# Five value groups and new images for q and k in a 16-batch attention and feed-forward kernel on one core

## The reference

```python
qkv = encodings @ attn_w.T + attn_b                      # (16, 256, 384)
q, k, v = jnp.split(qkv by heads, 3, axis=-1)
scores = jnp.einsum('bhki,bhqi->bhkq', k, q) / math.sqrt(8)
scores = jnp.where(mask, scores, -10000.0)               # key <= query
probs = jax.nn.softmax(scores, axis=2)                   # over the keys
combined = jnp.einsum('bhkq,bhkl->bhql', probs, v)
x = layernorm(x + combined @ out_w.T + out_b)
# lhs = x, per row: round(lhs / scale) in -127..127, likewise rhs per column
x = layernorm(x + (q_lhs @ q_rhs) * lhs_scale * rhs_scale)
```

## Time and profile before

| | us |
|---|---|
| median of 3 runs | 268.69 |
| lowest, highest | 267.32, 268.91 |
| profiled execution, its own time | 268.74 |
| its span in the trace | 266.9 |
| TensorE busy | 227.1 |
| VectorE, ScalarE, GpSimd busy | 187.7, 184.8, 129.4 |

### The profile page before, as it was taken

One profiled execution on the slowest core, in us unless ns is written; L12 is line 12 of the kernel. 1 busy time (PEld: TensorE's weight loads), 2 busy tenths in 40 slices (PEclk: granted clock), 3 DMA queues, 4 the chain that ended last, 5 costly groups with the idle time before them and its releaser, 6 DMA issues.

```text
span 266.9 us, 8051 instructions
## 1 busy us (share of the span) xinstructions
PE 227.1 (85%) x2991; PEld 174.3 (65%) x2991; DVE 187.7 (70%) x529; ACT 184.8 (69%) x384; POOL 129.4 (48%) x255
## 2 busy tenths in 40 slices
PE   6366859999999999999999999999999999888710
PEld 3144547778786878687878787878777777666300
DVE  4726866768678787888888888888878878434631
ACT  4895236776877868686868686878787676788420
POOL 7514040506162837474656556564646434455664
PEclk9858798999999999999999999999999999999955
DMA  4397497474747373747566564647464701010001
GB/s 138 121 233 130 131 254 145 141 140 141 143 138 144 100 180 113 162 128 160 141 151 154 141 158 136 145 130 154 150 113 155 127 22 27 18 46 19 22 20 41
DMA packets 50887, 32.77 MB, mean 123 GB/s; under 512 B 7200, under 2 KB 50848, under 8 KB 50848
## 3 DMA queue, kind: packets, MB, share of 16 engines
q1 hardware_dynamic: 50704, 32.06, 49.2%
q10 hardware_dynamic: 144, 0.20, 0.3%
HBM read 17.17 MB, written 14.68 MB: 119 GB/s over the span
## 4 chain that ended last, share of the span: by engine, by line
PE 70%; ACT 10%; issue 5%; DVE 5%; POOL 4%; DMA 4%; SPq 1%; POOLq 0%; ACTq 0%; DVEq 0%
PE pv_bank L902 16%; PE dve_bank L866 14%; PE act_bank L866 12%; PE act_bank L923 5%; PE act_bank L870 5%; PE dve_bank L870 4%; ACT heads_t L525 3%; PE dve_bank L947 3%; PE act_bank L933 3%; PE dve_bank L965 3%; DMA k_stat<-imagek 2%; DVE part_max L670 2%; PE dve_bank L913 1%; PE act_bank L975 1%; ACT k_stat L565 1%
## 5 line engine op out<-in xcount | busy, mean ns | idle before, releaser
L487 ACT ACTIVATE probs<-act_bank 128x512 f32<-128x512 f32 x160 | 96.3, 603 | 46.7 <-PE act_bank L870 42.8
L670 DVE TRANSPOSE_TENSOR_REDUCE part_max<-dve_bank 128x16 f32<-128x512 f32 x160 | 110.4, 707 | 19.1 <-PE dve_bank L870 18.1
L866 PE MATMUL dve_bank<-q_move,k_stat 124*128 124x192 bf16 (+3 forms) x512 | 66.3, 245 | 8.8 <-DMA k_stat<-imagek 7.4
L866 PE MATMUL act_bank<-q_move,k_stat 128*128 128x192 bf16 (+3 forms) x512 | 62.3, 235 | 0.5 <-DMA q_move<-shift 0.5
L866 PEld LDWEIGHTS dve_bank<-q_move,k_stat 124*128 124x128 bf16 x512 | 40.6, 118 | 28.6 <-issue 11.1
L902 PE MATMUL pv_bank<-probs,v_stat 128*32 128x256 f32 (+3 forms) x1024 | 48.7, 305 | 9.1 <-ACT heads_t L525 9.1
L416 POOL TENSOR_TENSOR qk_rest<-qk_f,qk_parts 128x512 f32<-128x512 f32 x15 | 17.5, 1166 | 73.6 <-ACT qk_f L505 73.6
L866 PEld LDWEIGHTS act_bank<-q_move,k_stat 128*128 128x128 bf16 x512 | 43.9, 115 | 2.9 <-DMA q_move<-shift 1.0
L870 PE MATMUL dve_bank<-causal,identb 128*128 128x256 bf16 (+1 forms) x160 | 41.9, 262 | 0.0
L870 PE MATMUL act_bank<-causal,identb 128*128 128x256 bf16 (+1 forms) x160 | 40.7, 254 | 0.0
L902 PEld LDWEIGHTS pv_bank<-probs,v_stat 128*32 128x32 f32 x1024 | 23.9, 109 | 20.3 <-ACT heads_t L525 12.5
(11 more groups left out here) (92 smaller groups left out, 321.9 us busy)
## 6 DMA issues: line engine op xcount, KB each, us to landing
imageq<-qk_parts SPq DMA_DIRECT2D x32, 192.0 KB, 1.9
imagek<-qk_parts SPq DMA_DIRECT2D x32, 192.0 KB, 2.0
q_move<-imageq SPq DMA_DIRECT2D x32, 192.0 KB, 3.9
k_stat<-imagek SPq DMA_DIRECT2D x32, 192.0 KB, 4.3
xt_in<-xt_dram SPq DMA_DIRECT2D x16, 128.0 KB, 4.3
x_in<-x_dram SPq DMA_DIRECT2D x16, 128.0 KB, 3.4
out_dram<-o SPq DMA_DIRECT2D x16, 128.0 KB, 2.0
q_move<-shift SPq DMA_DIRECT2D x32, 8.0 KB
```

The lines of the kernel that those rows point to most:

```text
L487: act.activation(probs[u][:, :], act_bank[at % ACT_BANKS][:, :], ACT.Exp, scale=SCALE).then_inc(act_emptied, 1)
L670: dve.tensor_reduce(out32, dve_bank[at % DVE_BANKS][:, :].rearrange("k (c q) -> k c q", q=32), op=ALU.max, axis=AX.X, apply_transpose=True ...
L866: pe.matmul(bank[:, at:at + TOK - blk * KB], keys, q_move[b % QK_RING][0:rows, p, blk * KB:TOK], start=(at == 0), stop=False, skip_group_c ...
```

## The change

The **images** are new. q's image has three planes (one per part) of 16 x 8 rows, ordered by head-in-pair and depth first and pair second, each of 256 values and 32 of padding. k's image has three planes of the same rows with the keys of both heads, 512 values and 32 of padding; the zeros of the other head are in the image (`zero_image` clears it once). A batch writes a q and a k plane for each part, six copies, and reads two products at a time, 32 rows, in six copies. Where both products use the same part, the source names the plane twice.

**Batch 0** does not go through an image: 12 copies of 16 rows bring it from SBUF to SBUF (`place_first`), k from `k_apart`, in which GpSimd has put the heads apart. Five of these copies are issued by ScalarE.

**q and k** are taken from the banks once, in fp32; GpSimd casts the first part. The weights of q and k are reordered once in SBUF (`wqk`). The third part is made at the start of GpSimd's next phase.

**Order in a phase.** `LEAD` is 6. There are five value groups of two units each. Products in fp32 stand together after units 1, 3, 5, 7 and 9; q and k are projected apart, after units 3 and 5; `project_out` moves one batch earlier, to the end of the phase before. The set-up of the feed-forward weights moves into phase -1. The ones and zeros of the last rows are written by VectorE and ScalarE in place of SyncE's four copies.

```diff
+PRODUCTS = ((0, 0), (2, 0), (0, 1), (0, 2), (1, 0), (1, 1))
+NPROD, ROWS = len(PRODUCTS), 2 * HD
+FIRST_LOADS, READS, WRITES = 2 * NPROD, NPROD, 2 * PARTS
+
+PAD = 32
+Q_PAIR, K_PAIR = TOK + PAD, 2 * TOK + PAD
+K_PLANE = ROWS * PAIRS * K_PAIR
+LAST_ROW, SHIFT_ROW = NPROD * ROWS, 124
...
-LEAD = 8
+LEAD = 6
...
-PV_GROUPS = [(0, 1), (2, 3, 4), (5, 6), (7, 8, 9)]
+PV_GROUPS = [(u, u + 1) for u in range(0, NU, 2)]
...
-ACT_EXTRAS = {0: [("v", 1)], 1: [("zq", -3)], 6: [("q", 4), ("k", 4)], 8: [("heads", -1)]}
-DVE_EXTRAS = {0: [("out", -2)], 4: [("ffn", -3)], 5: [("shift", 1), ("pv", -1)]}
+ACT_EXTRAS = {1: [("v", 1), ("zq", -3)], 3: [("q", 4)], 5: [("k", 4)], 7: [("heads", -1)]}
+DVE_EXTRAS = {4: [("ffn", -3)], 5: [("pv", -1), ("shift", 1)], 9: [("out", -1)]}
...
-        image = [[nc.dram_tensor(f"image{w}{i}", (128, NPROD, TOK), BF16, kind="Internal").ap()
-                  for i in range(QK_RING)] for w in "qk"]
+        q_image = [nc.dram_tensor(f"q_image{i}", (PARTS, ROWS * PAIRS, Q_PAIR), BF16, kind="Internal").ap()
+                   for i in range(QK_RING)]
+        k_image = [nc.dram_tensor(f"k_image{i}", (PARTS * K_PLANE + 2 * TOK,), BF16, kind="Internal").ap()
+                   for i in range(QK_RING)]
...
+        def place_first(eng, product, w):
+
+            q_part, k_part = PRODUCTS[product]
+            row = ROWS * product
+            if w == 0:
+                eng.dma_start(q_move[0][row:row + ROWS, :, :], qk_parts[0][:, q_part, 0, :]).then_inc(first_loaded, 16)
+            else:
+                eng.dma_start(k_stat[0][row:row + ROWS, :, :, :], k_apart[:, k_part, :, :]).then_inc(first_loaded, 16)
...
-            def write_image(b, half):
-
-                if not real(b):
-                    return
-                wait(sp, qk_split, b, 3 + half)
-                if b == 0:
-                    wait_place(sp, act_emptied, ACT_AT, ("k", b))
-                if half == 0:
-                    wait_ring(sp, qk_loaded, b - QK_RING, 4, 4)
-                for w in range(2):
-                    at = RUNS[w][half]
-                    sp.dma_start(image[w][b % QK_RING][:, 3 * half:3 * half + 3, :],
-                                 qk_parts[b % 2][:, at:at + 3, :]).then_inc(image_written[b % QK_RING], 16)
+            def zero_image(i):
+
+                blocks = k_image[i][0:PARTS * K_PLANE].rearrange("(r a q) -> r a q", r=128, q=K_PAIR)[:, :, 0:2 * TOK]
+                sp.dma_start(blocks, warm[:, :].unsqueeze(1).to_broadcast([128, PARTS, 2 * TOK])).then_inc(image_zeroed[i], 16)
+
+            def write_image(b, n):
+
+                if not real(b) or b == 0:
+                    return
+                if n == 0:
+                    wait_split(sp, b, 1)
+                    wait_loaded(sp, b - QK_RING)
+                    if b <= QK_RING:
+                        sp.wait_ge(image_zeroed[b % QK_RING], 16)
+                else:
+                    wait_split(sp, b, 2 + n)
+                half = K_PLANE // 2
+                k = k_image[b % QK_RING][n * K_PLANE:n * K_PLANE + 2 * (half + TOK)].rearrange("(s e) -> s e", s=2)
+                k = k[:, 0:half].rearrange("s (x q) -> s x q", q=K_PAIR)[:, :, 0:TOK]
+                sp.dma_start(q_image[b % QK_RING][n, :, 0:TOK],
+                             qk_parts[b % 2][:, n, 0, :]).then_inc(image_written[b % QK_RING], 16)
+                sp.dma_start(k, qk_parts[b % 2][:, n, 1, :]).then_inc(image_written[b % QK_RING], 16)
+
+            def two_of(planes, parts, size):
+
+                a, b = parts
+                if a == b:
+                    return planes[a, :, 0:size].unsqueeze(0).to_broadcast([2, ROWS * PAIRS, size])
+                return planes[a:b + 1:b - a, :, 0:size]
 
             def read_image(b):
-                if not real(b):
-                    return
-                wait_ring(sp, image_written, b, 4, 4)
+                if not real(b) or b == 0:
+                    return
+                wait_written(sp, b)
                 wait_place(sp, act_filled, ACT_AT, ("exp", b - QK_RING, NU - 1))
                 slot = b % QK_RING
-                for s in range(2):
-                    rows = slice(s * ROWS, (s + 1) * ROWS)
-                    q = image[0][slot].rearrange("(p s i) r q -> s (i r) p q", s=2, i=HD)
-                    k = image[1][slot].rearrange("(p s i) r q -> s (i r) p q", s=2, i=HD)
-                    sp.dma_start(q_move[slot][rows, :, :], q[s]).then_inc(qk_loaded[slot], 16)
-                    sp.dma_start(k_stat[slot][rows, :, s, :], k[s]).then_inc(qk_loaded[slot], 16)
+                k = k_image[slot][0:PARTS * K_PLANE].rearrange("(n x q) -> n x q", n=PARTS, q=K_PAIR)
+                for product in range(0, NPROD, 2):
+                    rows = slice(ROWS * product, ROWS * (product + 2))
+                    q_two, k_two = zip(*PRODUCTS[product:product + 2])
+                    sp.dma_start(q_move[slot][rows, :, :], two_of(q_image[slot], q_two, TOK)).then_inc(qk_loaded[slot], 16)
+                    sp.dma_start(k_stat[slot][rows, :, :, :], two_of(k, k_two, 2 * TOK)).then_inc(qk_loaded[slot], 16)
...
-                write_image(b + 3, 1)
+                if b == -3:
+                    place_first_batch()
+                    zero_image(1)
+                write_image(b + 3, 2)
                 if b < 0:
                     load_shift(b + 1)
                 read_image(b + 3)
-                if b == -2:
-                    set_shift_rows()
                 load_xt(b + 5)
                 if b >= 0:
                     load_shift(b + 1)
                 load_x(b)
+                if b in (-2, -1):
+                    zero_image(b + 4)
                 write_image(b + 4, 0)
+                write_image(b + 4, 1)
+                if b == -1:
+                    zero_image(0)
...
-                    wait(pool, qk_split, b - 1)
+                    wait_written(pool, b - 2)
+                    if b == 2:
+                        wait_loaded(pool, 0)
+                    pool.tensor_copy(first, qk_f[:, :, :]).then_inc(split_of(b), 1)
+                    wait_split(pool, b, 1)
+                    wait_split(pool, b - 1, 4)
                     pool.tensor_tensor(qk_rest[:, :, :], qk_f[:, :, :], first,
-                                       ALU.subtract).then_inc(qk_split[1], 1)
-                    pool.tensor_copy(first_again[b % 2], first).then_inc(qk_split[1], 1)
+                                       ALU.subtract).then_inc(split_of(b), 1)
                 else:
-                    wait(pool, qk_split, b, 3)
+                    wait_split(pool, b, 3)
                     pool.tensor_tensor(third, qk_rest[:, :, :], second,
-                                       ALU.subtract).then_inc(qk_split[1], 1)
+                                       ALU.subtract).then_inc(split_of(b), 1)
...
             def phase(b):
+                split(b + 3, True)
                 norm_factors(b - 2, 0, y_stats, rstd_made)
                 add_bias(b - 1)
                 add_residual(b - 3)
                 split(b + 4, False)
                 norm_factors(b - 3, 1, r_stats, rstd2_made)
                 norm2(b - 3)
-                split(b + 4, True)
...
-                src = act_bank[at % ACT_BANKS][:, 0:TOK]
-                first, whole = part[b % 2][0][:, w, :], qk_f[:, w, :]
+                src, dst = act_bank[at % ACT_BANKS][:, 0:TOK], qk_f[:, w, :]
                 if w == 1:
-                    src = src.rearrange("c (b k) -> c b k", b=4)
-                    first, whole = (d.rearrange("c (k b) -> c b k", b=4) for d in (first, whole))
-                act.activation(first, src, ACT.Identity, bias=bias[:, w:w + 1])
-                act.activation(whole, src, ACT.Identity, bias=bias[:, w:w + 1]).then_inc(act_emptied, 1)
+                    src, dst = src.rearrange("c (b k) -> c b k", b=4), dst.rearrange("c (k b) -> c b k", b=4)
+                act.activation(dst, src, ACT.Identity, bias=bias[:, w:w + 1]).then_inc(act_emptied, 1)
...
+                act.wait_ge(k_apart_made, 2)
+                for product in (0, 1, 4):
+                    place_first(act, product, 1)
+                act.wait_ge(k_apart_made, 4)
+                for product in (2, 5):
+                    place_first(act, product, 1)
...
                     exponentials(b, u)
-                    if u == 0:
+                    if u == 1:
+                        pv_from_psum(b - 1)
                         v_from_psum(b + 1)
-                    if u == 1:
                         zq_from_psum(b - 3)
-                    if u == 3:
-                        pv_from_psum(b - 1)
+                    if u == 3 and b > -4:
+                        qk_from_psum(b + 4, 0)
                     if u == 4:
                         norm1(b - 2)
-                    if u == 6 and b > -4:
-                        qk_from_psum(b + 4, 0)
+                    if u == 5 and b > -4:
                         qk_from_psum(b + 4, 1)
```

(55 more changed lines are left out.)

177 lines of the change are left out of this document (106 added, 71 removed).

## The result

The changed kernel takes **528.45 us** (median of 4 runs, 527.71 to 529.23) where the kernel before takes 268.5 us (4 runs, 267.32 to 268.91): a ratio of **1.970, with an interval of 1.963 to 1.977**. The profiled execution took 528.77 us for a span of 527.0. Now and then an execution of one and the same kernel is over 1.5% slower than its fastest; the ratios in this document leave such executions out, the times in us are medians of all.

The account below looks back on a forecast made before the run. TensorE's pass, 13.6 us a batch, bounds the kernel before; narrow copies on two engines would bound the changed one: 99 + 12 x 29.5 + 54.4 = 507 us of span, 509 us forecast; own range 445 to 612, stretched to 263 to 590.

Parts of the forecast that it names:

- The bound of before: Kernel before, middle batches: each costs one TensorE pass, 13.6 us, with TensorE working 13.14 of 13.70 us.
- Two engines for a 2 on either side: Image copies: four reads and three k writes a batch, with outermost count 2 on one side, run on two DMA engines.
- Bytes and rate: Two narrow-copy engines: 504 kB each per batch at 19.0 GB/s takes 26.5 us, with ends of 22.6 and 32.9.
- Round trip, 3 us: Between image writes landing and reads: about 3 us a batch not moving, making the cycle 29.5 us, not 13.6.
- The wait behind it: SyncE's queue: the shift of b+1 stands behind the reads of b+3, so phase b+1 starts when those are through.
- The start: Batches 0 to 3 through the images: phase 1 starts at 99 us (88 to 118), not 49.4.
- The end: Last three batches and the closing chain: 54.4 us, as in the kernel before.
- TensorE's side, covered: TensorE: `heads_t` wait of 9.1 us goes, five value groups add 9.1; in sum -2 to -3, covered by waiting.
- The sum of 266 for spread copies: Whole kernel if all copies use 16 engines: TensorE's sum holds, 268.7 - 2.5 = 266, say 263 to 270 us.
- Rivals 1 to 3: Copies spread over 16 engines: 266 us (chance 0.16), 259 by cheap value groups (0.10), 277 by late shift (0.08).
- rival 3: Copies spread, but the shift copy behind 1.18 MB of reads comes some 0.7 us late a batch: 277 us; chance 0.08.
- the signs named: Profile after: shift or `k_stat` waits of some 15 us once a batch, DMA share 0.15 to 0.2, clock 1.2 GHz after gaps.

Follow-up runs that it names:

- third run: The changed kernel with only k's image writes cut in two, the four reads with a 2 at the source left as they were; 512.29 us.
- all-wide: The changed kernel with every image copy cut so that no side has an outermost count of 2, 24 issues a batch on SyncE; 342.19 us.
- interleaved kernel: The all-wide kernel with its six reads again, rows of two products alternating, images unpadded, 20 issues a batch on SyncE; 305.10 us.
- run with the clearings moved: The interleaved kernel with `xt_in`, `x_in` and all image clearings on ScalarE's queue and q's first two parts written by one copy; 284.55 us.
- best version here: The run with the clearings moved, with the shift copies also issued from ScalarE's queue, at unit 5; 283.47 us.

## Why the prediction was right, step by step

- **The bound of before**: right. With all copies wide and few issues, single cycles of 13.75 us come back, TensorE's own; their mean stays at 14.4 to 14.7.
- **Two engines for a 2 on either side**: right, to the packet, in seven kernels; the inference from the destination's side to the source's held.
- **Bytes and rate**: the term of 26.5 us was close for a reason that was half right. In the window in which the narrow copies move alone, 47 GB/s at a share of 0.14 are 21 GB/s per engine, above my 19.0; but the shift's 64-byte pieces are slow (from 259 to 262 us 17 to 36 GB/s together), and 504 kB over the cycle less its pauses (some 27.5 us) come to 18.3. That 26.5 + 3 is within 0.5 us of the cycle is in part luck. Without k's narrow writes (third run) the two engines carry 86 kB less, 4.7 us at 18.3 GB/s, and the cycle is only 1.2 us shorter. In the cycle shown, the issues of the reads and of what follows up to `x_in` take 21.6 us, and the writes with their landing 8.4; in the second part SyncE's issues and the wait for the landing count, not the bytes alone.
- **Round trip, 3 us**: undersized. From the issue of the last write of k to the reads there are 5.0 us (265.01 to 269.98; 4.3 to 6.0 in the other cycles), where it landed in 2.0 before; with the writes narrow it stands in the same line. Part of that time the engines still move. The cycle is 30.03 for 29.5.
- **The wait behind it**: right, with one addition. SyncE's queue stalls on its own backlog, for some 16 us of the 30 beyond 0.6 us for each issue. I had named that as what would make the size wrong; it did not, because the queue stands still for as long as the two engines move. In the variants it decided twice: all-wide was bound by the queue's length, and one narrow read cost 3.7 us a batch.
- **The start**: the step that was off most, though inside its own bounds. Phase 1 began at 112.39, not 99 (88 to 118). Batch 0's scores, put near 15, began at 18.48, by the slow copies to neighbouring rows. Batch 1's reads were issued at 27.37 (20.5 forecast): its first write waited until 19.30 for the clearing of its image, issued at 13.43 and landed 5.8 us later, a wait that the sum did not have; part of it is the same slow copies, since the interleaved kernel's first write goes out at 16.75. The next two steps took 30.4 and 32.1 us (27.5 and 29 forecast). In each the first write again waits for a clearing (16.2 us over the three batches), and the reads come 5.2 and 6.0 us after the issue of the last narrow write.
- **The end**: 54.2 for 54.4. In sum 112.4 + 360.4 + 54.2 = 527.0, for 99 + 354 + 54.4 = 507.
- **TensorE's side, covered**: value groups 3.32 for 3.33, the wait on `heads_t` gone, the cast on GpSimd 609 ns, the lower of my bounds. The sum of 266 for spread copies was never reached: with spread copies this program needs more issues, its start stays longer, and single batches come late for a reason that is not settled. 283.5 is the best version here, and none beats the kernel before.
- **Rivals 1 to 3** had as their condition that the source's count does not matter. It does. What rival 3 names, a shift copy that comes late behind the wide reads, does show once the copies are wide: 9.6 us in nine waits in the run with the clearings moved.
- **The range**, 263 to 590, was stretched over the rivals and says little; the forecast's own, 445 to 612, holds the 528 too. Of the signs named, the waits on the shift (13 times, 14.9 us on average) and the clock came as told; the DMA share is 25%, not 15 to 20.
